# Issuing three bulk loads of a fused attention and mixture-of-experts kernel from ScalarE instead of SyncE

## What is computed

```
xn = layernorm(x)
q, k, v = split(xn @ w_qkv.T + b_qkv)
s = (softmax(q @ k.T / sqrt(512)) @ v) @ w_out.T + b_out
logits = xn @ router_w + router_b            # 8 experts, the best 2 of each token
h_e = silu(xn @ expert_w[e] + expert_b[e])   # 512 x 512 for each expert e
y = xn + (sum over the 2 experts of weight * h_e) @ proj_w + proj_b
g = silu(norm_w * y / rms(y))
```

## Time and profile before

| | |
|---|---|
| median of 3 runs | 568.08 us (562.79 to 569.07) |
| the profiled execution | 567.03 us |
| its span, first to last instruction | 565.1 us |
| TensorE busy | 525.4 us, 93% |
| VectorE / ScalarE / GpSimd busy | 286.8 / 188.2 / 201.7 us |
| bytes moved | 81.40 MB, mean 144 GB/s |
| median store of a slot tile, issue to landing | 2.0 us |

### The profile page before, as it was taken

How to read it: one execution, slowest core, us unless ns; L and a number is a source line. 1 busy time by engine, 2 the same in 40 slices (tenths; PEclk the granted TensorE clock), 3 DMA queues, 4 the chain that set the end, 5 groups by cost and what they waited for, 6 DMA issues and landing times.

```text
span 565.1 us, 7606 instructions
## 1 busy us (share of the span) xinstructions
PE 525.4 (93%) x2454; PEld 417.5 (74%) x2455; DVE 286.8 (51%) x444; ACT 188.2 (33%) x282; POOL 201.7 (36%) x312
## 2 busy tenths in 40 slices
PE   5827999899999999989899999999999999999996
PEld 2325747588878888768688888877888888888884
DVE  0973815357432833666344444445358564586552
ACT  0101313313103324444233333333265435155550
POOL 3530120000000587424233332063456767185243
PEclk9967999999999989989999999999999999999999
DMA  7518151400010048885744545497523443142202
GB/s 276 190 33 339 74 187 74 187 0 1 20 38 19 1 167 287 275 261 183 280 148 161 165 158 166 168 358 282 179 74 115 137 143 130 57 148 94 74 20 93
DMA packets 32795, 81.40 MB, mean 144 GB/s; under 512 B 3761, under 2 KB 3777, under 8 KB 32129
## 3 DMA queue, kind: packets, MB, share of 16 engines
q1 hardware_dynamic: 23520, 52.70, 26.0%
q0 software_dynamic: 7376, 24.93, 14.1%
q10 hardware_dynamic: 1872, 3.41, 2.1%
HBM read 56.13 MB, written 24.90 MB: 143 GB/s over the span
## 4 chain that ended last, share of the span: by engine, by line
PE 72%; DMA 13%; DVE 8%; POOL 2%; ACT 1%; issue 1%; SPq 1%; DVEq 0%; ACTq 0%; POOLq 0%
PE ab L1322 16%; PE ab L1324 16%; PE ab L1323 16%; PE tp L1328 7%; PE sc L1322 5%; PE sc L1324 5%; PE sc L1323 5%; DMA xb<-in_expert_w 3%; DMA xg<-xn_scratch 2%; DMA y_scratch<-yt 2%; DMA xb<-in_x 2%; POOL W L580 2%; DMA xn_scratch<-xn 2%; DMA s_scratch<-so 1%; PE ab L1362 1%
## 5 line engine op out<-in xcount | busy, mean ns | idle before, releaser
L1322 PE MATMUL ab<-W,st_h 128*128 x156 | 65.2, 418 | 5.9 <-DVE st_l L1049 5.9
L1324 PE MATMUL ab<-W,st_l 128*128 x156 | 61.8, 396 | 0.0
L1323 PE MATMUL ab<-W,st_h 128*128 x156 | 61.3, 393 | 0.0
L793 ACT ACTIVATE yt<-yt 128x512 f32<-128x512 f32 x39 | 24.7, 633 | 82.6 <-DVE yt L1191 82.6
L1322 PE MATMUL sc<-xt_h,t_h 128*128 128x512 f32 x128 | 51.1, 399 | 0.0
L1324 PE MATMUL sc<-xt_h,t_l 128*128 128x512 f32 x128 | 50.4, 394 | 0.0
L1323 PE MATMUL sc<-xt_l,t_h 128*128 128x512 f32 x128 | 50.3, 393 | 0.0
L620 POOL DMA_INDIRECT y<-y_scratch,pos x32 | 32.5, 1017 | 43.7 <-DMA y_scratch<-yt 20.6
L1049 DVE TENSOR_TENSOR st_l<-tp,st_h 128x512 fp32r<-128x512 f32 x40 | 27.7, 691 | 39.0 <-ACT st_h L789 38.8
L574 POOL TENSOR_TENSOR tile_hot<-in_tile,ids 128x640 fp32r<-128x640 f32 x2 | 6.5, 3242 | 114.2 <-DVE in_tile L1105 114.2
L1191 DVE TENSOR_TENSOR yt<-ab,bias_e 128x512 f32<-128x512 f32 x39 | 27.0, 691 | 31.4 <-PE ab L1324 22.4
(11 more groups left out here) (257 smaller groups left out, 1270.4 us busy)
## 6 DMA issues: line engine op xcount, KB each, us to landing
y_scratch<-yt SPq DMA_DIRECT2D x39, 256.0 KB, 2.0
xb<-in_expert_w POOLq DMA_DIRECT2D x6, 1024.0 KB, 6.7
xb<-in_x SPq DMA_DIRECT2D x4, 1024.0 KB, 8.8
xn_scratch<-xn SPq DMA_DIRECT2D x16, 256.0 KB, 2.0
x<-in_x SPq DMA_DIRECT2D x16, 256.0 KB, 2.9
nw_scratch<-nw SPq DMA_DIRECT2D x1, 2048.0 KB, 12.7
mw_scratch<-mw SPq DMA_DIRECT2D x1, 2048.0 KB, 7.3
s_scratch<-so SPq DMA_DIRECT2D x8, 256.0 KB, 3.0
```

The costliest lines, as they stand in the source:

```text
L793: nc.scalar.activation(yt[:, h, :], yt[:, h, :], ACT.Silu).then_inc(silu_d, 1)
L1322: nc.tensor.matmul(dst, lh, rh, start=start, stop=False)
L1323: nc.tensor.matmul(dst, lh, rl, start=False, stop=False)
L1324: return nc.tensor.matmul(dst, ll, rh, start=False, stop=stop)
```

## The change

The bias load moves from SP to ACT, behind `pt_split(3)` and the wait for the last scores, ahead of `w_high(0)`. The load of the folded value weights moves from SP to ACT, behind `silu(7)` and ahead of ACT's loop, with the same two waits. The load of the folded key weights moves from SP to ACT, between `own_split` of row tile 42 and the copy `v_hi(1, 2)`, with its wait for the scratch store. Nothing else is changed.

```diff
@@ -424,12 +424,6 @@
             for j in range(GB):
-                if j == QB + 1:
-
-                    sp.wait_ge(s_done, GB)
-                    sp.dma_start(bias_e[:, :, :].rearrange("p e f -> p (e f)"),
-                                 expert_b.rearrange("e f -> (e f)").rearrange("(a n) -> a n", a=1)
-                                 .to_broadcast([P, E * D])).then_inc(be_in, 16)
                 sp.wait_ge(ab_read, 2 + U["a", 0, j] + 1)
                 sp.dma_start(s_g[j], so[:, j % 2, :]).then_inc(so_st[j % 2], 16)
@@ -445,9 +439,6 @@
             for i in range(PEEL):
                 store_y(i, i % 2)
-            sp.wait_ge(w_lo, LATE)
-            sp.wait_ge(nw_st, 16)
-            sp.dma_start(nw1[:, :, :, :].bitcast(F32), nw_d).then_inc(nw_in, 16)
             with sp.Fori(PEEL // 2, LOOPED // 2) as i:
@@ -463,8 +454,6 @@
             sp.wait_ge(ab_full, U["e", LAST] + 1)
-            sp.wait_ge(mw_st, 16)
-            sp.dma_start(mw1[:, :, :, :].bitcast(F32), mw_d).then_inc(mw_in, 16)
             for q in range(2):
                 sp.wait_ge(xn_st[q], 8 * G)
@@ -803,6 +792,9 @@
             act.wait_ge(s_done, GB)
+            act.dma_start(bias_e[:, :, :].rearrange("p e f -> p (e f)"),
+                          expert_b.rearrange("e f -> (e f)").rearrange("(a n) -> a n", a=1)
+                          .to_broadcast([P, E * D])).then_inc(be_in, 16)
             for m in range(AHEAD):
                 w_high(m)
@@ -816,6 +808,10 @@
                 if i in (0, 2):
                     load_next(BY_POOL + 1 + i // 2)
+
+            act.wait_ge(w_lo, LATE)
+            act.wait_ge(nw_st, 16)
+            act.dma_start(nw1[:, :, :, :].bitcast(F32), nw_d).then_inc(nw_in, 16)
             with act.Fori(PEEL // 2, LOOPED // 2) as i:
@@ -864,6 +860,9 @@
             for t in range(GB):
                 if t + 1 < GB:
                     own_split(SLOT_TILES + t + 1)
+                if t == 2:
+                    act.wait_ge(mw_st, 16)
+                    act.dma_start(mw1[:, :, :, :].bitcast(F32), mw_d).then_inc(mw_in, 16)
                 v_hi(1, t)
```

## The result

The changed kernel is slower: 573.18 us median of 20 runs against 569.47 us for 20 runs of the kernel before, 3.7 us more. The ratio is 1.0089 (95% interval 1.0057 to 1.0121), about 5 us, but it compares only executions within 1.5% of the fastest of their kernel, and as one execution before took 562.79 us, that leaves out 8 of the 20 before and 1 of the 20 after. The means of all twenty, 573.33 and 569.96 us, are 3.4 us apart (0.59%), so the loss lies between 3.4 and 5 us. The forecast was 567.5 us and no change that can be told. The profiled execution of the changed kernel spans 567.4 us against 565.1; as single executions of either kernel lie several us apart, the twenty runs say how much was lost, and the trace only where.

What follows compares the result with a forecast made beforehand. TensorE, busy 525.4 of 565.1 us, was taken as the bound. Terms +2.0 (biases), -0.6 (value weights), -1.4 (key weights) sum to 0.0 on 567.03 us; half the median's difference added gives 567.5, range 562.5 to 572.

Steps and rivals of the forecast that it cites:

- Part B: Value-weight load moved to ScalarE after tile 7's SiLU: net -0.6 us, ends -2.81 and +0.4.
- The stores of tiles 8 and 9 no longer stand in the same queue behind 2 MB: Value-weight move, gap at 276: of 2.81 us at most, 0.9 us counted as won.
- My upper end for the part: Value-weight move, worst case +0.4 us: the issue on ScalarE delaying the high split of tile 9's rows.
- The ratio in the earlier trace: At 269 to 273, gathers got 24 packets against 90 beside the value weights; a store would wait until these are through.
- My working of the turns between queues: Value-weight move: if queues alternate by packet, most of the gap is won, -2.5 us; left out of the sum.
- Part A: Bias load issued 8.3 us later on ScalarE: slows the next expert load, +2.0 us, ends -1.5 and +5.
- the return: At the first bias add, 1.2 of 1.79 us idle time regained because an attention store goes out earlier.
- The starving rival: Bias and expert loads hold q0 down until 236, second tile 5 us later, low clock added: 573 us; chance 0.13.
- Part C: Key-weight load issued 5.1 us later on ScalarE: row-load waits at 381 to 386 go, -1.4 us, ends -1.55 and +1.0.
- I give 0.15 us for that: Key-weight move: allowance of 0.15 us for gathers of expert outputs made late by meeting the weights.
- The escape of the stores: Stores and row loads freed by separate queues, next expert load not slowed: -5.5 us, 561.5 us; chance 0.17.
- That places are only exchanged: Shared DMA engines: store and rows come when they came, bias move costs its 2.0 us: 569.5 us; chance 0.15.

Runs made afterwards that it cites:

- e2: Only the value-weight load moved to ScalarE, against the kernel before: ratio 1.0060 (1.0028 to 1.0092).
- e5: Only the value-weight load on ScalarE, written one step later, behind tile 9's high split, against the kernel before: ratio 1.0052 (1.0025 to 1.0080).
- e1: Only the bias load moved to ScalarE, against the kernel before: ratio 1.0017 (0.9987 to 1.0048).
- e10: The changed kernel with the value weights in eight 256 KB loads on SyncE between slot stores; against the kernel before, ratio 0.9894 (0.9847 to 0.9940).
- e3: Only the key-weight load moved to ScalarE, against the kernel before: ratio 1.0006 (0.9971 to 1.0041).
- e9: Only the value-weight load on ScalarE, its issue waiting until tile 9's high split has ended, against the kernel before: ratio 0.9986 (0.9956 to 1.0015).
- e6: Only the value-weight load on ScalarE, scratch copy laid out with 2 KB rows instead of 16 KB, against the kernel before: ratio 1.0009 (0.9982 to 1.0035).

## Why the prediction was wrong, point by point

**Part B, the step that failed.** I had -0.6 us; e2 measured +0.6% of 569.75 us, +3.4 us (1.6 to 5.2). The step is "The stores of tiles 8 and 9 no longer stand in the same queue behind 2 MB". It took the store of tile 7 for safe ahead of the load, since the load is written behind `silu(7)`. The load's issue was set down at "about 264.6"; the store's own, 264.64 in the kernel before, was not set beside it, and at such a distance order is everything: what the old place gave for nothing, the store first and then the load, on one queue, was not counted as something that the change removes. My upper end for the part, +0.4, was the cost of the issue alone. In its place the runs show a wait of 5.8 us for tile 7's store (1.8 us more of TensorE's idle time) and a stretch at the low clock (1.7 us), 3.5 us together in the changed kernel's trace. The 1.7 us are of one execution; over many, the table above has 1.3 (e2) and 1.7 us (e5), hardly clear of nothing. The issue itself cost next to nothing: the split of tile 9 ran 0.60 us after the start of the SiLU, before 0.54 us.

The ratio in the earlier trace rows, 24 packets of gathers against 90 of the weights, was the right row, and I used it to say that a store beside the load doesn't fare better. I did not ask of it what happens to a store that now goes behind the load. My working of the turns between queues (B -2.5) was wrong in itself: the store has 128 packets of 2 KB and the load 128 of 16 KB, so with one packet each in turn the store lasts as long as the load. The turns are there in the traces (40 to 44 in e2), and what none of my rows showed are the 4 us before the store's first packet.

The Trainium skill ("Advanced Engine Details and Errata", Sequencer and Instruction Queues) has the rule that I missed: instructions for the engine are pushed into its queue, while control instructions are started by the sequencer itself. The section does not say on which side the issue of a transfer falls; e5's rows, 0.07 us behind the SiLU's start and ahead of an earlier split, agree with the second. Read so, the place "behind tile 7's SiLU" reads as "at its start", 0.6 us ahead of the store.

**Part A** was right in its mechanism. The bias load went out at 220.59 and not at 221.8, again at the start of the split that I had put it behind. The next expert load came at 232.6, 0.4 us under my 233 to 236. In the changed kernel's timeline:

```profile
220.59 1.02 ACT L754 CAST pt_h<-tp 128x1024 fp32r<-128x1024 f32 x1 [2.41 <-PE tp L1327]
220.59 0.36 ACTq L795 DMA_DIRECT2D bias_e<-in_expert_b  x1
...
232.62 2.00 ACT L787 CAST W<-xb 128x1024 fp32r<-128x1024 f32 x2 [5.55 <-DMA xb<-in_expert_w]
...
237.66 0.50 PE L1321 MATMUL ab<-W,st_h 128*128 x1 [2.10 <-DVE st_l L1048]
```

The gap before the second tile grew from 0.34 to 2.10 us, and the return came too, larger than I let it: the first add started at 237.43, before at 237.67, and the add of tile 2 at 245.63, before at 245.14. So +0.5 us in this trace against +2.0 in the sum; e1's ratio says +1.0 us, with -0.7 to +2.7. The starving rival was not idle talk: in e10's profile the same expert load, issued at 226.37, was waited for by 8.90 us, until 238.59, with TensorE idle for 1.98 and 3.26 us. It did not make e10 slower than the other kernels with pieces by an amount that its ratio shows.

**Part C** had the right gain and a return mis-sized. No row transpose waits any more (1.55 us gone), and the key weights are there when needed. But the term "I give 0.15 us for that" measured 0.88 us: the gathers of expert outputs, sharing with key weights that now start later, held VectorE and so TensorE up. One of them, issued at 376.50, took 11.48 us, where their median is 4.4.

```profile
388.01 0.75 DVE L1219 SCALAR_TENSOR_TENSOR y<-y,w 128x512 f32<-128x512 f32 x1 [1.11 <-DMA y<-y_scratch,pos]
...
389.42 0.50 PE L1321 MATMUL ab<-nw,xt_h 128*128 128x512 f32 x1 [0.88 <-DVE xt_l L1213]
```

That is -0.7 instead of -1.4 in the trace. e3's gap there was 1.4 us, nearly all of what was won, and its ratio is that of no change.

**The sum.** By the trace +0.5 (A) + 3.5 (B) - 0.7 (C) = +3.3 us; the twenty runs of each kernel say 3.4 us by their means, 5 by the ratio (3.2 to 6.9). How near 3.3 comes is partly luck, since it holds the clock of single executions, whose spans differ by 2.3 us. The median of the kernel before was 569.47 over 20 runs and not 568.08, so the reference itself lay 1.4 us higher than I had it.

**The rivals.** The escape of the stores (0.17) is refuted by e2. That places are only exchanged (0.15) holds for B in e9, the form in which the order of store and load is kept. My slower rival was placed in the wrong part: the outcome on that side came from the mechanism that I had named for A, a bulk load holding up a smaller transfer on another queue, at a place where I had the store down as passed.

## What to carry to other kernels

A transfer that is moved to another engine's queue loses its order against everything that was issued ahead of it in the old queue: list what stands *before* it there, not only what stands behind it. In this kernel a load of 2 MB next to stores with two buffers was a stall in either queue. Cut into pieces the size of the stores (256 KB here) and laid between them, by either issuer, it left no idle time in 266 to 284, and 0.9 to 1.1% came back. Read issue times on an engine that also computes from the queue rows, since an issue can come ahead of the engine's own earlier work; where it must come behind, it needs a wait on that work's semaphore.

## What was unexpected of the hardware

A transfer issue on ScalarE overtook ScalarE's own earlier datapath instruction: 266.17 against 266.64 in e5, and 220.59 for a load written behind a split that ran from 220.59 to 221.61. And a transfer that comes 0.6 us behind 2 MB on another queue waits about 4 us for its first packet, with packets of 16 KB (e2: issued at 264.04, none before 268) as with 2 KB (e6: issued at 266.11, none before 270); the turns between the queues, 40 packets to 44 in e2, begin only then. The store that went 0.48 us ahead, in e9, landed in 2.4 us altogether. Why the first packet takes so long was not tried.
